# Column sums of the kept diagonal blocks added up on GpSimd instead of VectorE

## The reference

```python
# layer 0
adj_hat = adj + jnp.eye(8192)
d_inv_sqrt = 1.0 / jnp.sqrt(jnp.sum(adj_hat, axis=1))
out = (adj_hat * d_inv_sqrt[:, None] * d_inv_sqrt[None, :]) @ (x @ W0) + b
x = layernorm(x + relu(out))
# layer 1
support = x @ W1
o = relu(support + adj @ support + x @ Wself)
x = layernorm(x + pair_norm(o))
```

## Time and profile before

| | us |
|---|---|
| median of 3 runs | 1895.53 |
| lowest and highest run | 1893.96, 1898.31 |
| the profiled execution | 1895.76 |
| its span in the trace | 1893.9 |
| mean granted clock of TensorE | 0.982 |

### The profile page before, as it was taken

One profiled execution on the slowest core, in us unless ns is written; L12 is line 12 of the kernel. 1 busy time (PEld: TensorE's weight loads), 2 busy tenths in 40 slices (PEclk: granted clock), 3 DMA queues, 4 the chain that ended last, 5 costly groups with the idle time before them and its releaser, 6 DMA issues.

```text
span 1893.9 us, 20444 instructions
## 1 busy us (share of the span) xinstructions
PE 1732.6 (91%) x7682; PEld 1407.2 (74%) x7682; DVE 1454.3 (77%) x1898; ACT 1208.8 (64%) x1644; POOL 21.5 (1%) x34
## 2 busy tenths in 40 slices
PE   1089999999999999989999999999989999999983
PEld 0077778888887888767788888888868888877862
DVE  4486688686878679976777575665589999999987
ACT  3576687576856646645555454454478888888865
POOL 0000000000000000100000000000000000000001
PEclk9999999999999999999999999999999999999995
DMA  9999999999899487944445445545589999999933
GB/s 397 422 421 421 421 383 421 395 394 399 352 365 374 187 344 297 335 178 156 156 178 178 178 175 185 196 172 186 198 316 389 385 386 387 386 376 369 384 151 89
DMA packets 80290, 572.02 MB, mean 302 GB/s; under 512 B 8960, under 2 KB 8960, under 8 KB 12096
## 3 DMA queue, kind: packets, MB, share of 16 engines
q1 hardware_dynamic: 76608, 557.88, 74.7%
q0 software_dynamic: 3584, 12.85, 2.2%
HBM read 566.49 MB, written 4.19 MB: 301 GB/s over the span
## 4 chain that ended last, share of the span: by engine, by line
PE 76%; DVE 11%; DMA 6%; ACT 4%; issue 2%; SPq 1%; POOL 0%; ACTq 0%; DVEq 0%
PE acc L1010 18%; PE acc L1012 18%; PE acc L1016 18%; PE pC L992 5%; PE pD L992 5%; DMA zr<-in_adjN 4%; DVE raw_low L705 4%; ACT hi L532 2%; DMA s<-in_adjT 1%; DMA raw<-in_adjT 1%; DVE o_low L705 1%; PE pA L1010 1%; DVE zr_low L705 1%; PE pB L1010 1%; PE pA L1012 1%
## 5 line engine op out<-in xcount | busy, mean ns | idle before, releaser
L705 DVE TENSOR_TENSOR raw_low<-raw,hi 128x1024 fp32r<-128x1024 f32 x578 | 687.3, 1220 | 90.8 <-ACT hi L532 86.5
L1010 PE MATMUL acc<-hi,rhi 128*128 128x512 f32 x1792 | 719.1, 401 | 36.0 <-DVE raw_low L705 15.1
L532 ACT ACTIVATE hi<-raw 128x1024 fp32r<-128x1024 f32 x578 | 596.4, 1055 | 180.0 <-PE pD L992 76.6
L1016 PE MATMUL acc<-hi,rlo 128*128 128x512 f32 x1792 | 555.3, 391 | 0.0
L1012 PE MATMUL acc<-raw_low,rhi 128*128 128x512 f32 x1352 | 529.5, 392 | 0.0
L1010 PEld LDWEIGHTS acc<-hi,rhi 128*128 128x128 f32 x1792 | 338.3, 189 | 127.2 <-DVE raw_low L705 24.8
L1016 PEld LDWEIGHTS acc<-hi,rlo 128*128 128x128 f32 x1792 | 338.3, 189 | 72.4
L1012 PEld LDWEIGHTS acc<-raw_low,rhi 128*128 128x128 f32 x1352 | 255.4, 189 | 54.9 <-issue 3.6
L705 DVE TENSOR_TENSOR zr_low<-zr,hi 128x1024 fp32r<-128x1024 f32 x144 | 173.1, 1222 | 41.1 <-ACT hi L532 38.6
L704 DVE TENSOR_TENSOR rlo<-zr,rhi 128x256 fp32r<-128x256 f32 x123 | 52.0, 423 | 174.8 <-ACT hi L532 174.8
L532 ACT ACTIVATE hi<-zr 128x1024 fp32r<-128x1024 f32 x144 | 151.3, 1060 | 53.8 <-PE pD L992 22.5
(11 more groups left out here) (186 smaller groups left out, 1807.4 us busy)
## 6 DMA issues: line engine op xcount, KB each, us to landing
raw<-in_adjT SPq DMA_DIRECT2D x289, 1024.0 KB, 5.0
zr<-in_adjT SPq DMA_DIRECT2D x72, 1024.0 KB, 5.3
raw<-in_adjN SPq DMA_DIRECT2D x66, 1024.0 KB, 18.2
o<-in_adjT SPq DMA_DIRECT2D x32, 1024.0 KB, 10.9
s<-in_adjT SPq DMA_DIRECT2D x27, 1024.0 KB, 15.1
zr<-in_adjN SPq DMA_DIRECT2D x25, 1024.0 KB, 22.2
s<-in_adjN SPq DMA_DIRECT2D x21, 1024.0 KB, 19.4
s<-in_xT POOLq DMA_DIRECT2D x8, 512.0 KB, 6.5
```

The costliest lines, as they stand in the source:

```text
L532: S.activation(hi[n % DEEP][:, :], slice_of(chunk, j), ACT.Copy).then_inc(hi_ready, 1)
L705: V.tensor_sub(low_of(chunk, j), slice_of(chunk, j), hi[n % DEEP][:, :].bitcast(f32)).then_inc(slice_split, 1)
L1010: T.matmul(banks[h][:, :], a, hi[n % DEEP][:, part], start=opens, stop=False, skip_group_check=True)
L1016: last = T.matmul(banks[h][:, :], b, hi[n % DEEP][:, part], start=False, stop=end, skip_group_check=True)
```

## The change

`sum_kept` moves from VectorE's program to GpSimd's, with the same adds and the same waits. GpSimd runs it for stage 0 behind its constants, and for stage k behind its load of xT for that stage. VectorE's list does nothing at a kept chunk.

```diff
@@ block.gpsimd @@
+            def sum_kept(chunk):
+                k, q = chunk.row, chunk.q
+                pool.wait_ge(*landed(chunk))
+                if q == 0:
+                    if k > 0:
+                        pool.wait_ge(sums_closed, k)
+                    pool.tensor_add(colsum, slice_of(chunk, 0), slice_of(chunk, 1)).then_inc(col_step, 1)
+                    return
+                for j in range(JB):
+                    pool.wait_ge(col_step, k * (JB * Q - 1) + q * JB + j - 1)
+                    pool.tensor_add(colsum, colsum, slice_of(chunk, j)).then_inc(col_step, 1)
...
+            kept_chunks = [c for c in chunks if c.kind == "keep"]
+            for chunk in kept_chunks[:Q]:
+                sum_kept(chunk)
             for k in range(1, NB):
                 pool.wait_ge(y_done, k * H)
                 pool.dma_start(xT_blk, xT[:, k * BLK:(k + 1) * BLK]).then_inc(xT_in, 16)
+                for chunk in kept_chunks[k * Q:(k + 1) * Q]:
+                    sum_kept(chunk)
@@ block.vector @@
-            def sum_kept(chunk):
...
                 if chunk.kind == "keep":
-                    sum_kept(chunk)
                     continue
```

## The result

| | before | after |
|---|---|---|
| median, us | 1895.62 | 1923.97 |
| lowest and highest run, us | 1893.96, 1898.31 | 1923.87, 1924.87 |
| span of the profiled execution, us | 1893.9 | 1923.1 |

The ratio is 1.0148 with an interval from 1.0136 to 1.0161: the change makes the kernel 28 us slower. The forecast was 1930, in a range from 1896 to 1960.

The account below looks back on a forecast made before the run. From stage 2 on TensorE, busy 91% overall, was taken to bound the kernel. Stages 2 to 4 (10.5 us), 5 (7.8), 6 and 7 (16.2) sum to 34.5, added to 1895.76: 1930 us, range 1896 to 1960.

Parts of the forecast that it names:

- The disputed cost: GpSimd adds beside VectorE splits in phase 1: they exclude each other and take turns, 34.5 us in all, chance 0.60.
- Rival 1: GpSimd and VectorE don't disturb each other: splits stay at 1.22 us, stage 5 regains 3.6 us, 1892.2 us; chance 0.16.
- rival 3: Add costs 2.3 us but blocking is softer than turns: between 0 and half of 34.5 us, 1896 to 1913; chance 0.12.
- rival 2: Exclusion, but two VectorE splits go between adds, so sums come late at the closes: about 1907 us; chance 0.12.
- The add: One 128x1024 f32 add on GpSimd: 2.3 us, the middle of 1.6 and 3.1 us.
- The turn: Split 1.22 plus add 2.3 plus handover 0.1: 3.6 us per split against TensorE's 2.3, losing 1.3 us per split.
- The lead: Time from a split's end to its use by TensorE, taken off the loss: 4.3 us in stage 2, 0.5 in cached blocks.
- Stage 0: Adds behind the first four loads: GpSimd done near 20 us, ScalarE reads the sums at 24.9; cost nothing.
- Stage 1: Paced by the DMA, with 11 us of idle TensorE: costed at nothing, 3.5 us if loads start later.
- Stage 5: Adds falling partly into the cached block cost 11.4 us, less 3.6 recovered by the removal: 7.8 us.
- the granted clock: TensorE's clock, 1.00 in stages 2 to 7: if it fell after the new waits, that would come on top; no size.
- Stages 6 and 7: First add hits the cached block: 2.3 + 7.8 less some 2 us of lead, 8.1 us each, 16.2 together.

Follow-up runs that it names:

- all four variants: The changed kernel with its GpSimd adds on 8 columns, on 512 columns, replaced by copies, or replaced by two memsets each: 1893.4, 1895.5, 1894.8 and 1893.5 us.
- the removal by itself: The changed kernel with the 56 GpSimd adds on 8 of 1024 columns, the rest of the sums left out: 1893.4 us, ratio 0.999 to the kernel before.
- the pace that bites: The changed kernel with GpSimd adds of stages 2 and 3 waiting for higher TensorE slice counts, so they stand about 4.6 us apart: 1916.4 us, ratio 1.0108.
- the first pace: The changed kernel with adds of stages 2 and 3 also waiting for two more multiplied slices each, counts TensorE had mostly passed: 1924.5 us, ratio 1.0156.
- the first experiment: The same run as the removal by itself: the changed kernel with the GpSimd adds on 8 of 1024 columns, 1893.4 us.

## Why the prediction was right, and where its terms were off

- The disputed cost. I took exclusion with turns, because a split reads two streams at full rate at once. The exclusion held: copy and add exclude splits, the memset does not. That the rate of reading is the reason no run tests; shown is only which pairs exclude each other. The rule of the Trainium skill (SBUF — State Buffer, section Who interferes with whom), that a VectorE instruction with two SBUF inputs excludes a GpSimd instruction that reads SBUF but not one that only writes, agrees with all four variants: longest split 3.43 us beside adds, 2.11 beside copies, 1.23 beside memsets. Rival 1 (1892 us) and rival 3 (up to 1913) fall by the time, rival 2 (about 1907) by the time and by the trace: nearly every add let one split through, not two.
- The add: 2.3 us as estimated, 2.34 measured, with luck. The 1.46 ns per element of the earlier trace rows gave 1.6 us for one input, and a copy took 1.05; by it the second input would add 0 or 1.5 us, and it added 1.3. The middle of the two ends was a choice without a row behind it.
- The turn: 3.6 forecast, 3.35 measured, though add and split make 3.56. Nothing goes to a handover, and adjoining VectorE instructions overlap by 0.08 us; the other 0.13 us are not accounted for. So the excess over TensorE's pace is 1.05 us per split and not 1.3.
- The lead. By those sizes stage 2 should have cost 6.3 - 4.3 = 2.0 us and not 3.3. The missing part is what I had put down as fitting into GpSimd's turns: the reduce at 283.25 took its 2.27 us right before the burst. So the split behind it, itself held up by 0.5 us, ended 3.8 us after its forerunner (287.16) and had 2.3 us of lead left, as its slice starts at 289.44. The five splits after it come every 3.34 us against 2.27: 5.4 us lost, less 2.3, is 3.1, what the close shows. The additions to ux did fit. In stages 2 and 4 the two errors nearly cancelled, by luck: 3.3 each against 3.5. In stage 3 they did not: 4.8.
- Stage 0: I had GpSimd done near 20 us and in time for ScalarE at 24.9. I had counted only the last pair behind the last load; but six adds of 2.34 us stand in a row from 9.18 on and end at 23.74, and ScalarE read 2.8 us later. The forecast cost of nothing still came out, as the close of stage 1 isn't later.
- Stage 1: 0 forecast, -0.2 measured; the DMA paces it.
- Stage 5: 7.8 forecast, 6.9 measured. The removal gives 2.3 us, not 3.6, because I had counted the wait for o_low to the column sums; the adds then cost 9.1 us there (the closes of stages 4 and 5 against those of the removal by itself), not 11.4. And the granted clock dropped in this burst, which the prediction had named as a thing that would come on top. From 605 to 612 it was half, 1.2 in place of 2.4 GHz, in the middle of TensorE's waits:

```profile
605.00:612.00 7.00, 5.39 (x13) 3.32 (x12) 7.00 (x3) 2.11 (x2) 6.78 (x3) 0.51 0.77 305
```

  It did not come on top. In the run with the pace that bites, stage 5 has the same adds on GpSimd, its burst stands 7.9 us earlier, and the clock stayed at 1.00 through the same part of it:

```profile
597.00:604.00 7.00, 3.67 (x15) 2.39 (x14) 7.00 (x3) 2.11 (x2) 6.78 (x3) 1.00 0.96 358
```

  Slices start 3.3 us apart in both (599.53, 602.86 and 606.20 there; 607.37, 610.68 and 614.01 in the changed kernel), and stage 5 adds 7.0 us there against 6.9. At either clock TensorE was done with a slice before the next split came.
- Stages 6 and 7: the terms that were furthest off, 8.1 each against 5.4 and 4.2. I let the first add take its turn in the cached block, at 2.3 us of TensorE's time; instead it waited 3.3 and 6.2 us and let splits through. Of stage 7 this left GpSimd late: its last add ends at 780.96, and TensorE waits 0.6 us at the close, a piece of rival 2.
- Sum: 34.5 forecast, 27.7 at the last close. The mechanism was right and the sum 6.8 us too high, most of it in stages 6 and 7. The span ends 29.1 us later; the rest arises behind phase 1, and the run with the first pace, whose last close is 27.8 us late, ended 26.3 us later. I take that 1 to 2 us for scatter between executions.

No version here beats the kernel before beyond its interval. The trace of the first experiment shows why: taking the sums off altogether moves the last close by 2.3 us, 0.12%, and with the rest of the program as it is no other place for them can give more.

## What to carry to other kernels

VectorE's share of busy time said nothing about this move: the engine relieved was ahead of TensorE in all stages but one, and the engine that took over the work stopped it. Before work with SBUF inputs goes to GpSimd, lay its instructions beside VectorE's two-input ones: add both lengths to a turn and compare it with the time in which the bounding engine uses up one result. Below it the blocking was free here, above it each turn cost the excess as soon as the lead was gone. So the spacing of the same adds took 8 us off, and half-width adds cost only the 2.1 us of stage 5, where a slice is used up in 1.4 us.

## What the runs showed of the hardware

- An f32 add on GpSimd of 128 x 1024 with two SBUF inputs takes 2.34 us alone, 128 x 512 1.28, 128 x 8 0.19; a copy of 128 x 1024 1.05, a memset 0.95.
- The length of an instruction in the profile includes the time in which it is shut out: 3.42 us for a split of 1.22, 8.56 for an add of 2.34. The waiting isn't shown as idle time, so both engines look busier than they are. A mean that moves (1220 to 1347 ns) is the sign.
- In a burst, turns are strict, one split to one add; but the first add of a stage was overtaken by two (stage 6) and by five (stage 7) splits in a row.
